# Third norm's first tiles turned through DRAM, and the first routed tiles' rows turned and signalled earlier

## The chip, the cores and the metric

The kernel runs on one core of one Trainium2 chip. The metric is the device time of one execution in microseconds; before the change it was 700.5 us in the median of three runs (699.7 to 701.65).

## What is computed

The input x has 16 x 64 = 1024 tokens of 512 numbers; a context of the same shape goes with it. Four blocks follow each other, each added to x:

```python
x = x + _L0_xattn_ref(_layernorm(x), ctx, ctx)            # linear attention, heads of 8 channels
x = x + _L0_ffn_ref(_layernorm(x), U1, V1, U2, V2, b1, b2) # low rank 128, inner width 1376
x = x + _L1_xattn_ref(_layernorm(x), ctx, Wq, Wk, Wv, Wo)  # 16 heads, 4 key/value heads of 96
x = x + _L1_ffn_ref(_layernorm(x), gate_w, bias, Wg, Wu, Wd, Sg, Su, Sd)
# the last one: scores = sigmoid(x @ gate_w.T) + bias; the best 4 of 16 experts of each token,
# weights normed to sum 1; out = sum over them of w * (silu(x@Wg.T) * (x@Wu.T)) @ Wd.T,
# plus a shared expert silu(x@Sg.T) * (x@Su.T) @ Sd.T
```

All is fp32. The experts have an inner width of 256.

## The kernel before

The 1024 tokens are 8 tiles of 128 rows (j = 0 to 7); x stays in SBUF as `xr`. One Python list, `prog`, holds all steps up to the routed experts in one order (lines 282 to 400), and each engine walks it and issues its own part of each step. So the order within each engine is written by hand, and semaphores join the engines.

The **second attention** is 32 units, n = 0 to 31, two per batch (lines 369 to 393). Unit n has on TensorE: the scores `s(n)` (8 matmul records, L1366), one large piece (a q projection `q`, an output projection half `op0`/`op1` of L1397, or a shared-expert piece `sh_gu`), the transposes `t(n-1)` of the probabilities (L1195), and `pv(n-2)` (L1382). VectorE has in it the largest score (L1038, L1040), `pn(n)` (L852, L853), the copies of q (L1029) and of pv (L1054, L1056). ScalarE has the exponentials (L746) and the copy of the transposes (L668). TensorE's pv(n) waits until VectorE has copied pv(n-1).

Once a tile j of x is final after `op1`, the **third norm** starts beside these units, placed by the table WAY (lines 353 to 357): `ln_stat` (VectorE L943, L944, then GpSimd's root, L562, L563), `ln_z` (VectorE writes the normed rows to one of two `zrow` buffers, L1001), `ln_t` (TensorE turns them in four 128x128 transposes, ScalarE copies them to `zT`, L668), `gate` (TensorE's scores for 16 experts), `gate_v` (VectorE's choice of the best four, L1078 to L940), and `place` (TensorE's running counts, then VectorE's slot numbers, L1108 to L1110). With the slot numbers GpSimd scatters the four copies of each row from `zrow` to `slot_rows` in DRAM (L601, four indirect DMAs for a tile), and writes token ids and weights to `slots` (L569, four more).

The **second norm** has another way to the same layout (lines 491 to 500 and 1003 to 1008): SyncE stores `zrow` to DRAM, loads it again in four quarters into `zquad`, and VectorE's 32x32 block transposes finish it (L1007).

After unit 31 come the last norms, the shared expert's products (`sh_gu`, `sh_d`; VectorE adds each of the eight `sh_d` to `xr`, L1130), and the tables of the routing, which ScalarE copies to `tab` (L790). Then come some 36 **routed tiles** of 128 slots. For each one the rows are loaded from `slot_rows` by four DMAs (`load_block`, L425; for tile 0 `load_first_block`, L431), turned by VectorE (`turn`, L925), and go through gate and up, a transpose, and down on TensorE; GpSimd adds the result to the output by an indirect DMA (L635).

SyncE's queue at that handover holds, in order: the first block's four loads, the wait for the load table, the wait for `tab`, the four loads of block 1, the two signals `s_w` that say that the weights of the first two experts are there (L530, L531), the eight stores of the output, and the loads of further experts. TensorE's first routed tile (`gate_up(0)`) waits for `s_w` and for the first turn. VectorE has turn 0 ahead of the add of `sh_d` 6 and turn 1 ahead of the add of `sh_d` 7 (L1126, L1127). TensorE waits for `tab` ahead of the last shared product, `sh_d` 7.

Of the kernel before, what the change touches and what calls it, by code (L numbers as in the profile page):

```python
# [29 lines left out]
PIECES = EW // D  # L30
EARLY = 4
WARM = 12
EPS = 1e-5
# [3 lines left out]
def build(nc, x_d, ctx_d, ctxT_d, cst_d, u1_d, v1_d, u2_d, v2_d, b1_d, b2_d,  # L37
# [10 lines left out]
    with ExitStack() as stack:  # L48
# [155 lines left out]
        s_x1 = sem("x1_done")  # L204
        s_z = sem("z_done")
        s_zst = [sem(f"second_norm_stored{i}") for i in range(2)]
        s_zld = sem("second_norm_loaded")
# [132 lines left out]
        for i, u in enumerate(lat_units[0][2:]):  # L340
# [7 lines left out]
            if i in (1, 3, 4):  # L348
# [3 lines left out]

        tail_of = ((10, 1, "ln_z"), (11, 2, "ln_t"), (12, 1, "gate"), (13, 1, "place"))
        WAY = [((7, 0, "op0"), (9, 0, "op1"), (9, 1, "ln_stat")) + tail_of,
               ((7, 0, "op0"), (8, 0, "op1"), (9, 1, "ln_stat")) + tail_of,
               ((6, 0, "op0"), (7, 0, "op1"), (7, 1, "ln_stat"), (8, 1, "ln_z"), (9, 2, "ln_t"), (9, 1, "gate"),
# [12 lines left out]
        for n in range(NU + 1):  # L369
            if n < NU:  # L370
                prog.append(("s", n))
            prog += [("gate_v", step[1]) for step in prog[since:] if step[0] == "gate"]
            since = len(prog)
            if n == 14:
                prog.append(("gate_b", 0))
            if n < len(lat_units[1]):
                prog.append(("kv", lat_units[1][n]))
            for j in BESIDE.get(n, ()):
                prog.append(("sh_gu", j))
            if n < NU:  # L380
                prog.append(("pn", n))
            q, r = n // 8, n % 8
            if q < 3 and r % 2 == 0:
                prog.append(("q", q + 1, r // 2))
            way(n, 0)
            if 1 <= n <= NU:
                prog.append(("t", n - 1))
            way(n, 2)
            if 2 <= n <= NU + 1:
                prog.append(("pv", n - 2))  # L390
            way(n, 1)
            if n == 13:
                prog.append(("front",))
# [6 lines left out]
                 ("sh_d", 4), ("sh_d", 5), ("sh_d", 6), ("sh_d", 7)]  # L400

        def order(kinds):
            return {step: i for i, step in enumerate(p for p in prog if p[0] in kinds and p[:2] != ("ln_t", 2))}

# [16 lines left out]

        def load_block(eng, block_of, par, landed):

            for b in range(4):
                eng.dma_start(xrow[b * QD:(b + 1) * QD, par, :].rearrange("p (a e) -> p a e", a=4),  # L425
                              quads_d[bass.ds(block_of, 1), b, :, :, :].rearrange("x j a e -> (x j) a e")).then_inc(landed, 16)
# [22 lines left out]
        def _(sp):  # L449
# [86 lines left out]
            with sp.Fori(2, loads) as o:  # L536
# [118 lines left out]
        def _(act):  # L655
# [15 lines left out]
            for step in prog:  # L671
# [18 lines left out]
                elif kind == "a_t":  # L690
# [3 lines left out]
                    copied(step, ekT[:, j % 2, :])  # L694
                elif kind == "ln_t" and step[1] != 2:

# [103 lines left out]
            def x_load(i, par):  # L800
# [3 lines left out]
                load_block(act, block_of, par, s_gx[par])  # L804

            act.wait_ge(s_tabl, 1)
            act.wait_ge(s_tab, 1)
            tail = act.value_load(head[0:1, 4:5], min_val=28, max_val=TILES - 3)
# [32 lines left out]
        def _(dve):  # L841
# [104 lines left out]
            for step in prog:  # L946
# [39 lines left out]
                elif kind == "ln_z":  # L986
# [5 lines left out]
                    if n >= 2:  # L992
                        old = [p for p in prog if p[0] == "ln_z"][n - 2]
                        if old[1] == 2:
                            dve.wait_ge(s_zst[old[2] % 2], 16 * (old[2] // 2 + 1))
                        else:
# [6 lines left out]
                elif kind == "ln_t" and step[1] == 2:  # L1003
                    j = step[2]
                    dve.wait_ge(s_zld, 64 * (j + 1))
                    dve.wait_ge(s_pt, j // 4 + 1)
                    dve.transpose(zT[:, :, j * P:(j + 1) * P].rearrange("p k (a j) -> p a k j", a=4),  # L1007
# [110 lines left out]
                elif kind == "sh_gu" and step[1] >= EARLY and step[1] % 2:  # L1118
                    i = step[1]
                    a = i // 2  # L1120
                    dve.wait_ge(s_hsil, a + 1)
                    dve.wait_ge(s_hg, i + 1)
                    dve.tensor_tensor(zs[:, a, :], shared_bank(i), shg[a % 2], ALU.mult).then_inc(s_hz, 1)
                elif kind == "sh_d":
                    j = step[1]
                    if j >= J - 2:  # L1126
                        turn(j - (J - 2), j % 2)  # L1127
                    dve.wait_ge(s_hd, j + 1)
                    dve.wait_ge(s_x3, j + 1)
                    dve.tensor_tensor(xr[:, j, :], shared_down(j), xr[:, j, :], ALU.add).then_inc(s_x4, 1)  # L1130
# [42 lines left out]
        def _(pe):  # L1173
# [24 lines left out]
            def normed(layer, j):  # L1198

                if layer == 2:  # L1200
                    pe.wait_ge(s_zt2, j + 1)
                else:
# [18 lines left out]
            for step in prog:  # L1221
# [28 lines left out]
                elif kind == "kv":  # L1250
# [36 lines left out]
                elif kind == "ln_t" and step[1] != 2:  # L1287
                    n = LNN[("ln_z", *step[1:])]
# [338 lines left out]
```

## Time and profile before

| | |
|---|---|
| median of three runs | 700.5 us |
| the profiled execution | 706.84 us, its span 704.7 us |
| TensorE busy | 678.4 us, 96% |
| VectorE, ScalarE, GpSimd busy | 346.1, 193.4, 176.4 us |
| chain that ended last | TensorE 80%, VectorE 7%, DMA 6% |
| mean granted TensorE clock | 0.991 |

The first 76 us hold the first attention, then the low-rank network runs to about 158 us, the projections to 194 us, the units of the second attention from 194 to 445 us, the shared expert to 489 us, and the routed tiles from 492 us on. Times are counted from the first instruction of the span. A DMA row of a queue gives the time for issuing, not for the transfer.

### The profile page before, as it was taken

Reading aid. Unit: us, or ns where it says so; the run is one execution under the profiler, and the core shown is the slowest. Engines: PE = TensorE matmul, PEld = TensorE weight load, DVE = VectorE, ACT = ScalarE, POOL = GpSimd, SP = SyncE. Lnnn points to the kernel's source line nnn. Section 1 sums busy time; section 2 is a strip of 40 time slices with the busy share of each in tenths; the row PEclk is TensorE's granted clock in tenths of the full one; section 3 lists DMA queues with packets and bytes.
Section 4 is the critical chain, followed back from the end, with each engine's and each line's share of the span. In section 5 each row is a group of like instructions: output and inputs, shape, how many; then the busy total and the mean of one; then the engine's idle time right before and its main releaser. Section 6 shows DMA issues by size and latency. Waiting matters only on the chain.

```text
span 704.7 us, 9742 instructions
## 1 busy us (share of the span) xinstructions
PE 678.4 (96%) x2460; PEld 403.3 (57%) x2461; DVE 346.1 (49%) x838; ACT 193.4 (27%) x543; POOL 176.4 (25%) x226
## 2 busy tenths in 40 slices
PE   9999999999999999999999999997999999999991
PEld 6555444446777776777776785674444444444440
DVE  3999232533344456576675767455333333333330
ACT  5452422222254332333333242220111111111110
POOL 2354210100000000013513314255033333433332
PEclk9999999999999999999999999999999999999997
DMA  9999998123310100001104105313767757868544
GB/s 338 408 421 420 422 421 331 45 75 134 116 50 0 57 34 0 1 21 41 60 2 150 60 2 170 129 75 88 265 165 136 168 98 180 187 137 233 94 65 58
DMA packets 60403, 103.19 MB, mean 146 GB/s; under 512 B 7200, under 2 KB 32544, under 8 KB 59712
## 3 DMA queue, kind: packets, MB, share of 16 engines
q1 hardware_dynamic: 30608, 73.61, 28.3%
q0 software_dynamic: 8816, 18.00, 12.7%
q10 hardware_dynamic: 20944, 11.15, 5.5%
q8 instruction: 18, 0.29, 0.2%
q14 instruction: 17, 0.14, 0.1%
HBM read 46.60 MB, written 56.26 MB: 146 GB/s over the span
## 4 chain that ended last, share of the span: by engine, by line
PE 80%; DVE 7%; DMA 6%; issue 2%; POOL 1%; ACT 1%; ACTq 1%; POOLq 1%; DVEq 0%; SPq 0%; another core or an unknown queue 0%
PE ps L1207 47%; PE ps L1397 12%; DMA out<-rq,sidx 5%; PE ps L1366 4%; PE ps L1382 4%; PE ps L1195 3%; DVE rq L975 3%; PE ps L1313 3%; PE ps L1314 3%; PE ps L1323 3%; PE ps L1335 1%; DMA xr<-in_x 1%; DVE st L943 1%; ACTq L425 1%; DVE zrow L1001 1%
## 5 line engine op out<-in xcount | busy, mean ns | idle before, releaser
L1207 PE MATMUL ps<-kv,rq 128*128 x432 | 194.1, 598 | 4.1 <-DVE rq L925 3.5
L1207 PE MATMUL ps<-zT,r 128*128 128x256 f32 (+1 forms) x552 | 132.6, 395 | 1.5 <-ACT kv L708 1.4
L1207 PEld LDWEIGHTS ps<-kv,rq 128*128 128x128 f32 x432 | 79.6, 191 | 92.0 <-issue 91.4
L1207 PEld LDWEIGHTS ps<-zT,r 128*128 128x128 f32 x552 | 103.4, 190 | 25.4 <-issue 12.0
L1397 PE MATMUL ps<-r 128*128 128x512 f32 x192 | 85.1, 593 | 0.0
L635 POOL DMA_INDIRECT out<-rq,sidx x36 | 56.7, 1574 | 112.0 <-DMA out<-rq,sidx 81.4
L562 POOL TENSOR_SCALAR ve<-mv 128x1 f32<-128x1 f32 x32 | 7.2, 224 | 292.6 <-DVE mv L944 292.6
L746 ACT ACTIVATE r<-ps,snm 128x128 f32<-128x128 f32 x128 | 45.3, 366 | 83.3 <-DVE snm L1040 79.8
L1134 DVE TENSOR_TENSOR rq<-ps,rq 128x256 f32<-128x256 f32 x36 | 15.3, 424 | 96.8 <-ACT rq L798 93.8
L1397 PEld LDWEIGHTS ps<-r 128*128 128x128 f32 x192 | 35.2, 190 | 38.3 <-issue 38.3
L798 ACT ACTIVATE rq<-ps 128x256 f32<-128x256 f32 x36 | 13.8, 384 | 126.5 <-PE ps L1207 105.9
L1145 DVE TENSOR_SCALAR rq<-ps,wts 128x512 f32<-128x512 f32 x36 | 27.0, 750 | 33.3 <-PE ps L1207 13.1
L601 POOL DMA_INDIRECT slot_rows<-zrow,sloti x32 | 33.5, 1046 | 35.0 <-DVE sloti L1110 26.8
L1029 DVE COPY rq<-ps 32x256 f32<-32x256 f32 x48 | 20.5, 427 | 41.5 <-PE ps L1207 41.0
L1016 DVE SCALAR_TENSOR_TENSOR rq<-ps,r,rq 128x512 f32<-128x512 f32 (+1 forms) x22 | 16.4, 749 | 40.3 <-ACT rq L727 40.3
L668 ACT COPY r<-ps 128x512 f32<-128x512 f32 x40 | 23.4, 586 | 45.3 <-PE ps L1195 42.7
L1366 PE MATMUL ps<-kv,rq 96*128 96x128 f32 x256 | 34.8, 279 | 0.0
L1382 PE MATMUL ps<-r,kv 128*96 128x256 f32 x128 | 32.9, 379 | 1.3 <-DVE r L1056 1.3
L569 POOL DMA_INDIRECT slots<-tokw,sloti x32 | 31.3, 977 | 10.4 <-issue 9.2
L1366 PEld LDWEIGHTS ps<-kv,rq 96*128 96x128 f32 x256 | 32.6, 192 | 1.4
L1054 DVE COPY r<-ps 96x192 f32<-96x192 f32 x64 | 19.8, 349 | 19.8 <-PE ps L1382 19.2
L1056 DVE COPY r<-ps 32x128 f32<-32x128 f32 x96 | 27.5, 287 | 1.3
(176 smaller groups left out, 843.3 us busy)
## 6 DMA issues: line engine op xcount, KB each, us to landing
slot_rows<-rq SPq DMA_DIRECT2D x4, 8192.0 KB, 50.2
kv<-in_experts SPq DMA_DIRECT2D x54, 256.0 KB
rq<-slot_rows ACTq DMA_DIRECT2D x136, 64.0 KB
r<-in_Wq SPq DMA_DIRECT2D x1, 3072.0 KB, 10.3
r<-in_Wo SPq DMA_DIRECT2D x2, 1536.0 KB, 6.4
r<-in_ctx SPq DMA_DIRECT2D x8, 256.0 KB, 8.3
xr<-in_x SPq DMA_DIRECT2D x8, 256.0 KB, 8.4
second_norm_rows<-zrow SPq DMA_DIRECT2D x8, 256.0 KB, 2.1
```

The costliest lines, as they stand in the source:

```text
L569: pool.indirect_dma_start(out=id_d.rearrange("a (b c) -> (a b) c", c=2), out_offset=bass.IndirectOffsetOnAxis(ap=sloti[:, j, k:k + 1], axi ...
L601: pool.indirect_dma_start(out=slot_d, out_offset=bass.IndirectOffsetOnAxis(ap=sloti[:, j, k:k + 1], axis=0), in_=zrow[:, LNN[("ln_z", 3, j ...
L635: pool.indirect_dma_start(out=out_d, in_=ylast[:, par, :] if last else yrow[:, par, :], in_offset=None, out_offset=bass.IndirectOffsetOnAx ...
L668: act.copy(dst, ps[:, n % 2, :] if len(dst.shape) == 2 else ps[:, n % 2, :].rearrange("p (k t) -> p k t", k=KC)).then_inc(s_trc, 1)
L746: e = act.activation(prob[:, n % 2, u, :], ps[:, 2 + n % 2, u * P:(u + 1) * P], ACT.Exp, bias=snm[:, n % 4, u:u + 1], scale=SCALE, accum_o ...
L975: link(dve.reciprocal(srec, ps[:, 5, :]))
L1056: c = dve.tensor_copy(dst[HD:P, :, t, :], src[32 * t:32 * t + 32, :, 3, :])
L1145: dve.tensor_scalar(ylast[:, par, :] if last else yrow[:, par, :], ps[:, 6 + par, :], wts[:, bass.ds(col, 1)], None, ALU.mult).then_inc(s_ ...
L1207: mm = pe.matmul(out, lhs(k), rhs(k), start=(k == 0), stop=(k == n - 1))
L1366: mm = pe.matmul(ps[:, 2 + n % 2, u * P:(u + 1) * P], qT[0:HD, q % 2, b % 4, h0:h0 + 2, :].rearrange("p h s -> p (h s)"), kT[0:HD, g, b, : ...
L1382: mm = pe.matmul(ps[0:HD, 6, 256 * g:256 * g + 256], v[:, b, c0:c0 + HD], probT[:, n % 2, 256 * g:256 * g + 256], start=True, stop=True)
L1397: mm = pe.matmul(ps[:, 7, :], oT[:, j % 2, m, :], wo[:, m, :], start=(m == 0), stop=(m == NQT - 1))
```

## The change

Third norm, tiles 0 to 4 (`TURNED = 5`): they go by DRAM and VectorE as the second norm does. VectorE writes the normed rows twice, once to `zrow` for GpSimd's scatter and once, with the 128-byte pieces in another order, to `zquad`. SyncE stores `zquad`, loads it again in quarters, and VectorE transposes it. The five TensorE transposes groups and ScalarE's five copies are gone. In the table, `ln_t`, `gate` and `place` of these tiles stand one unit later; `front` and `gate_b`, too. `gate` 4 and `gate` 5 now both stand in unit 29, their `gate_v` in unit 30. Tiles 0 to 3 of it stand on SyncE's queue ahead of the wait for all of q and the load of the shared weights, tile 4 behind it.

Handover: SyncE gives the two `s_w` signals before it waits for `tab`; of block 1 it loads two quarters, and ScalarE loads the other two on its own queue, ahead of its first `x_load`; SyncE reads the number of expert loads only behind the output stores. VectorE has turn 0 ahead of the add of `sh_d` 4.

```diff
+TURNED = 5
-        tail_of = ((10, 1, "ln_z"), (11, 2, "ln_t"), (12, 1, "gate"), (13, 1, "place"))
+        turned_of = ((10, 1, "ln_z"), (12, 1, "ln_t"), (13, 1, "gate"), (14, 1, "place"))
...
-            if n == 14:
+            if n == 15:
                 prog.append(("gate_b", 0))
...
-            if n == 13:
+            if n == 14:
                 prog.append(("front",))
...
+        def by_dram(step):
+            return step[0] == "ln_t" and (step[1] == 2 or step[1] == 3 and step[2] < TURNED)
...
             def turn_rows(j):
-                sp.wait_ge(s_z, LNN[("ln_z", 2, j)] + 1)
-                sp.dma_start(zrow_d[j % 2], zrow[:, LNN[("ln_z", 2, j)] % 2, :]).then_inc(s_zst[j % 2], 16)
+                z = LNN[("ln_z", 2 + j // J, j % J)]
+                sp.wait_ge(s_z, z + 1)
+                if j >= J:
+                    sp.wait_ge(s_zp, j - J + 1)
+                sp.dma_start(zrow_d[j % 2], zrow[:, z % 2, :] if j < J else zquad[:, :]).then_inc(s_zst[j % 2], 16)
...
             load_wo(1)
+            for j in range(4):
+                turn_rows(J + j)
             sp.wait_ge(s_q, 4 * G)
             sp.dma_start(wsh, ws_d).then_inc(s_ws, 16)
+            turn_rows(J + 4)
...
             load_first_block(sp)
-            sp.wait_ge(s_tabl, 1)
-            loads = sp.value_load(head[0:1, 2:3], min_val=TOPK, max_val=E)
-            sp.wait_ge(s_tab, 1)
-            load_block(sp, sp.value_load(tab[0:1, 1:2], min_val=0, max_val=P), 1, s_gx[1])
             for i in range(2):
                 sp.wait_ge(s_wdma[i], 16 * PIECES)
                 sp.sem_inc(s_w, 1)
+            sp.wait_ge(s_tab, 1)
+            load_block(sp, sp.value_load(tab[0:1, 1:2], min_val=0, max_val=P), 1, s_gx[1], range(2))
             for j in range(J):
                 sp.wait_ge(s_x4, j + 1)
                 sp.dma_start(out_d[j * P:(j + 1) * P, :], xr[:, j, :]).then_inc(s_out, 16)
-            sp.wait_ge(s_tab, 1)
+            sp.wait_ge(s_tabl, 1)
+            loads = sp.value_load(head[0:1, 2:3], min_val=TOPK, max_val=E)
...
+            act.wait_ge(s_tab, 1)
+            for k in range(TOPK):
+                act.wait_ge(s_zs[k], 16 * J)
+            load_block(act, act.value_load(tab[0:1, 1:2], min_val=0, max_val=P), 1, s_gx[1], range(2, 4))
...
+                    if layer == 3 and j < TURNED:
+                        dve.wait_ge(s_zt2, J + j)
+                        dve.tensor_scalar(zquad[:, :].rearrange("p (b k i) -> p k b i", b=4, k=KC),
+                                          xr[:, j, :].rearrange("p (k b i) -> p k b i", b=4, k=KC),
+                                          mv[:, col, 0:1], rstd[:, col:col + 1],
+                                          ALU.subtract, ALU.mult).then_inc(s_zp, 1)
...
                     j = step[1]
-                    if j >= J - 2:
-                        turn(j - (J - 2), j % 2)
+                    if j == J - 4:
+                        turn(0, 0)
+                    if j == J - 1:
+                        turn(1, 1)
                     dve.wait_ge(s_hd, j + 1)
```

TensorE's `normed` waits for the VectorE transposes (`s_zt2`) where a tile goes by DRAM, and for ScalarE's copy elsewhere; VectorE's `ln_t` waits for the loads of the tile.

## Rows read from the trace of the kernel before

**Rows 1.** The page: busy time of each engine, its share of the span, instructions.

```profile
PE 678.4 (96%) x2460; PEld 403.3 (57%) x2461; DVE 346.1 (49%) x838; ACT 193.4 (27%) x543; POOL 176.4 (25%) x226
```

**Rows 2.** Windows: each engine's busy time (instructions), granted clock, DMA share, GB/s.

```profile
330.00:360.00 30.00, 30.00 (x151) 22.77 (x150) 20.66 (x65) 10.64 (x42) 8.89 (x10) 1.00 0.09 36
492.00:498.00 6.00, 5.78 (x10) 2.53 (x11) 1.80 (x3) 0.35 (x1) 0.60 (x1) 0.72 0.93 327
```

**Rows 3.** Waits of TensorE, 440 to 560 us: total, times, longest.

```profile
PE ps L1207 <- DVE rq L925: 3.5, 1, 3.5
PE ps L1382 <- DVE r L1056: 1.3, 1, 1.3
```

**Rows 4.** Chain, 340 to 350 us: start, duration, what (t and ln_t together).

```profile
347.33 0.87 PE ps L1195 x8
```

**Rows 5.** By line: ns least/median/most, first and last start; landings of L494, L499.

```profile
L1007 DVE STREAM_TRANSPOSE zT<-zquad x8: 697/702/712, 139.5 to 195.7; 128x512 f32<-128x512 f32 x8
L1001 DVE TENSOR_SCALAR zrow<-xr,mv,rstd x24: 534/546/1267, 35.8 to 460.3; 128x512 f32<-128x512 f32 x24
DMA to landing us min/median/max: 2.0/2.1/2.2
DMA to landing us min/median/max: 1.8/1.9/2.9
```

**Rows 6.** Timeline of VectorE, units 29 to 31: start, duration, line, operation.

```profile
425.68 0.17 DVE L1078 TENSOR_SCALAR gsc<-gsc 128x16 f32<-128x16 f32 x1
428.29 0.44 DVE L940 TENSOR_SCALAR tokw<-top,wsum 128x4 f32<-128x4 f32 x1
433.56 0.69 DVE L1038 TENSOR_REDUCE smx<-ps 128x4 f32<-128x512 f32 x1
439.51 0.89 DVE L1056 COPY r<-ps 32x128 f32<-32x128 f32 x3
443.21 0.59 DVE L1001 TENSOR_SCALAR zrow<-xr,mv,rstd 128x512 f32<-128x512 f32 x1
```

**Rows 7.** Timeline of TensorE, there: start, duration, line, operation, idle before.

```profile
440.54 1.07 PE L1382 MATMUL ps<-r,kv 128*96 128x256 f32 x4 [1.26 <-DVE r L1056]
445.77 0.60 PE L1195 MATMUL ps<-cst,zrow 128*128 128x128 f32 x4
```

**Rows 8.** Timeline of GpSimd, there: scatters of tile 5, root of tile 6.

```profile
433.81 0.96 POOL L601 DMA_INDIRECT slot_rows<-zrow,sloti  x1 [3.31 <-DVE sloti L1110]
438.07 0.96 POOL L601 DMA_INDIRECT slot_rows<-zrow,sloti  x1 [0.30 <-issue]
441.43 0.23 POOL L562 TENSOR_SCALAR ve<-mv 128x1 f32<-128x1 f32 x1 [2.39 <-DVE mv L944]
```

**Rows 9.** Timeline of all engines at the handover, 480 to 496 us.

```profile
480.16 1.77 SPq L431 DMA_DIRECT2D rq<-slot_rows  x4
481.58 7.11 PE L1207 MATMUL ps<-r 128*128 128x512 f32 x16 [0.44 <-issue]
483.49 0.19 ACT L790 CAST tab<-ps 6x48 int32<-6x48 f32 x1 [9.05 <-remote]
486.96 3.94 SPq L425 DMA_DIRECT2D rq<-slot_rows  x4
489.87 1.45 DVE L1130 TENSOR_TENSOR xr<-ps,xr 128x512 f32<-128x512 f32 x2 [7.08 <-PE ps L1207]
491.24 0.70 DVE L925 STREAM_TRANSPOSE rq<-rq 128x512 f32<-128x512 f32 x1
494.10 0.71 DVE L925 STREAM_TRANSPOSE rq<-rq 128x512 f32<-128x512 f32 x1 [1.59 <-DMA rq<-slot_rows]
```

**Rows 10.** Chain, 480 to 706 us: start, duration, what.

```profile
501.26 3.45 PE ps L1207 x8
684.75 4.90 DMA out<-rq,sidx
693.15 1.57 POOL out L635
```

More of the change, by code:

```diff
@@ L205, in build @@
         s_z = sem("z_done")
+        s_zp = sem("z_permuted")
         s_zst = [sem(f"second_norm_stored{i}") for i in range(2)]
@@ L351, in build @@
         NU = 2 * B
-        tail_of = ((10, 1, "ln_z"), (11, 2, "ln_t"), (12, 1, "gate"), (13, 1, "place"))
-        WAY = [((7, 0, "op0"), (9, 0, "op1"), (9, 1, "ln_stat")) + tail_of,
-               ((7, 0, "op0"), (8, 0, "op1"), (9, 1, "ln_stat")) + tail_of,
+        turned_of = ((10, 1, "ln_z"), (12, 1, "ln_t"), (13, 1, "gate"), (14, 1, "place"))
+        WAY = [((7, 0, "op0"), (9, 0, "op1"), (9, 1, "ln_stat")) + turned_of,
+               ((7, 0, "op0"), (8, 0, "op1"), (9, 1, "ln_stat")) + turned_of,
                ((6, 0, "op0"), (7, 0, "op1"), (7, 1, "ln_stat"), (8, 1, "ln_z"), (9, 2, "ln_t"), (9, 1, "gate"),
@@ L400, in build @@
                  ("sh_d", 4), ("sh_d", 5), ("sh_d", 6), ("sh_d", 7)]
+        def by_dram(step):
+            return step[0] == "ln_t" and (step[1] == 2 or step[1] == 3 and step[2] < TURNED)
         def order(kinds):
-            return {step: i for i, step in enumerate(p for p in prog if p[0] in kinds and p[:2] != ("ln_t", 2))}
+            return {step: i for i, step in enumerate(p for p in prog if p[0] in kinds and not by_dram(p))}
         TRN = order(("a_t", "ln_t", "t", "gate", "front", "place", "count"))
@@ L420, in load_expert, with load_block @@
                              we_d[bass.ds(expert, 1), :, c * D:(c + 1) * D].rearrange("a p n -> (a p) n")).then_inc(landed, 16)
-        def load_block(eng, block_of, par, landed):
-            for b in range(4):
+        def load_block(eng, block_of, par, landed, parts=range(4)):
+            for b in parts:
                 eng.dma_start(xrow[b * QD:(b + 1) * QD, par, :].rearrange("p (a e) -> p a e", a=4),
@@ L694, in _ @@
                     copied(step, ekT[:, j % 2, :])
-                elif kind == "ln_t" and step[1] != 2:
+                elif kind == "ln_t" and not by_dram(step):
                     copied(step, zT[:, :, step[2] * P:(step[2] + 1) * P])
@@ L995, in _ @@
                             dve.wait_ge(s_zst[old[2] % 2], 16 * (old[2] // 2 + 1))
-                        else:
+                        elif not by_dram(("ln_t", *old[1:])):
                             dve.wait_ge(s_tr, TRN[("ln_t", *old[1:])] + 1)
@@ L1002, in _ @@
                                       ALU.subtract, ALU.mult).then_inc(s_z, 1)
-                elif kind == "ln_t" and step[1] == 2:
-                    j = step[2]
-                    dve.wait_ge(s_zld, 64 * (j + 1))
-                    dve.wait_ge(s_pt, j // 4 + 1)
+                    if layer == 3 and j < TURNED:
[4 more added lines that the diff above has]
+                                          ALU.subtract, ALU.mult).then_inc(s_zp, 1)
+                elif by_dram(step):
+                    j = step[2]
+                    dve.wait_ge(s_zld, 64 * (J * (step[1] - 2) + j + 1))
+                    if step[1] == 2:
+                        dve.wait_ge(s_pt, j // 4 + 1)
+                    else:
+                        dve.wait_ge(s_q, 4 * (j // 2) + 4)
+                        dve.wait_ge(s_pr, len(KVN))
                     dve.transpose(zT[:, :, j * P:(j + 1) * P].rearrange("p k (a j) -> p a k j", a=4),
@@ L1198, in normed @@
             def normed(layer, j):
-                if layer == 2:
-                    pe.wait_ge(s_zt2, j + 1)
+                if by_dram(("ln_t", layer, j)):
+                    pe.wait_ge(s_zt2, J * (layer - 2) + j + 1)
                 else:
@@ L1286, in _ @@
                               lambda k: weights[1][:, k, :], KC).then_inc(s_pr, 1)
-                elif kind == "ln_t" and step[1] != 2:
+                elif kind == "ln_t" and not by_dram(step):
                     n = LNN[("ln_z", *step[1:])]
```

1 line of the change is left out of this document (removed).

## The prediction

> **What bounds the kernel now.** I read the page's busy times first: TensorE is busy 96% of the span, the next engine 49% [rows 1]. So only two things can move the time: TensorE work that goes or comes, and the few places where TensorE stands. The windows by stage say where the second kind is. A window in the middle of the second attention has TensorE busy for 30.00 of 30 us, beside VectorE at 20.7 and ScalarE at 10.6 [rows 2]: TensorE sets the pace there, and VectorE has about a third of its time free. The waits of TensorE after 440 us name two stalls: 1.3 us for a copy of pv (L1056), and 3.5 us for the first routed turn (L925) [rows 3].
>
> The second one is the larger target, so I read its surroundings in the timeline [rows 9]. The four last shared products run from 481.58 to 488.69. The first routed product starts at 492.22 (turn 0 ends at 491.94, the timeline has it at 491.24 for 0.70). Turn 0 stands on VectorE behind the adds of `sh_d` 4 and 5, and VectorE, idle for 7.08 us, got to these only at 489.87, though the first of the products should by the records be done some 2 us after 481.58. SyncE gives the `s_w` signals behind its four loads of block 1: the loads were issued from 486.96 to 490.90, though `tab` was there at 483.68. These four loads took 3.94 us to issue where the four of the first block took 1.77. Whatever delayed both engines there, both things that TensorE needs were queued behind it. After the stall the granted clock was 0.72 in the window 492 to 498 [rows 2], a mean over the upper level (2.4 GHz) and the lower (1.2 GHz), and TensorE had stood for 3.5 us before it fell.
>
> **The change, part by part.**
>
> *Third norm, TensorE.* Eight transposes, four of `t` and four of `ln_t`, take 0.87 us of the chain [rows 4], so a tile's four take 0.435 us. Five tiles: -2.2 us, in a stage where TensorE never stands, so all of it counts. The copies that ScalarE loses were hidden.
>
> *Third norm, VectorE.* Each of five tiles adds one more normed write and one transpose. The transpose is 0.70 us; the write to `zrow` is 0.55 us [rows 5]. No row has the write with the other order of pieces: I take 0.55 us (same count of elements, contiguous pieces), at most the 1.27 us of the slowest of the 24 [rows 5], at least 0.53. So 1.25 us for a tile, 6.2 us in all. A tile has four units, some 31 us of TensorE, where VectorE has over 9 us free [rows 2]; that hides it on average. The fullest unit becomes n = 18 (as 22): the gate's choice, 3.05 us (L1078 at 425.68 to the end of L940 at 428.73 [rows 6]), moves to where the q copies and both writes are. It overfills that unit by 2 to 3 us. The next unit holds only scores, probabilities and pv copies, and TensorE has its 5-us piece before it needs pn: nothing. If that cover were gone, each of the four such units would cost up to 2 us.
>
> *The round trip.* The store lands 2.1 us after its issue, the loads 1.9 us [rows 5], with issuing in between some 6 us. VectorE's transpose comes two units (15 us) after the write and the gate one unit after that: nothing. On SyncE's queue the wait stands ahead of the load of the shared weights; tile 3's rows are written in unit 22, where q is finished too, and the shared weights are needed three units later: nothing. Behind VectorE's new wait stands the reduction of the next scores, so a late landing would reach TensorE; from 6 us to 15 us there is room.
>
> *The end of the units.* `gate_v` 4 and 5 both come in unit 30. TensorE's place of 5 needs the second one, and gets it about 0.8 us before its turn. But the reduction of the scores 31 (433.56 before) moves behind two slot computations, and the chain reduction, exponential, pn 31, copies of pv 29 moves with it. The pv copies end at 440.40 before (L1056 [rows 6]), and TensorE, which waits for them, starts at 440.54 after 1.26 us of idle [rows 7]: I put this copy 0.55 us later. Then GpSimd: its four scatters of tile 5 start at 433.81, and the root of tile 6 at 441.43 finds it free [rows 8]. After the change the scatters of 4 and 5, eight at 1.3 us, start near 434.4 and end near 445, the root follows, and `ln_z` 6 (443.21 before [rows 6]) ends near 446.9. TensorE's transposes of tile 6 started at 445.77 [rows 7], now 446.3 with the delay above: another 0.55 us. Together +1.1 us, bounds 0 and 3 (if VectorE comes a further 2 us late). The third norm nets -1.1 us.
>
> *Handover.* Turn 0 now waits only for its rows, which were issued at 480.16 to 481.93; at the worst landing of block 1 (issued until 490.90, turned at 494.10 [rows 9], so 3.2 us) they are there by 486. `s_w` comes before the wait for `tab`. So `gate_up(0)` can start when the last shared product ends, at 488.69: -3.5 us. It runs 3.45 us (eight products [rows 10]), to 492.1. `gate_up(1)` needs turn 1, still ahead of the add of `sh_d` 7. Two loads each on two queues take 1.97 us to issue at the measured 3.94 us for four: from 486.96 to 488.9, landed 3.2 us later at 492.1, turned at 492.8, TensorE at 493.1. A new stall of 0.9 us. Its bounds: nothing if the issue is as quick as the first block's 1.77 us, 3 us if the delay stays as large as it was. With the short idle the clock should not fall: 6 us at 0.72 [rows 2] lost 1.7 us, which come back. The handover nets -3.5 + 0.9 - 1.7 = -4.3 us, bounds 0 and -5.2. The output stores and the later expert loads move with it; the two further loads on ScalarE stand ahead of its first silu, which is idle till then.
>
> *Sum.* -1.1 - 4.3 = -5.4 us on the profiled execution, 706.84 to 701.4 us. The median of the runs lies 6.3 us below that execution. Is the handover's stall in the timed runs? In the chain the last scatter-add starts at 693.15, and the one before that of which the landing is seen took 4.90 us [rows 10]; so work ends at about 698, and 6.7 us of the span and 2.1 us around it hold no work. The 6.3 us fit there. They would also fit the stall, the clock and 0.6 us of small gaps (5.8 us), if these came from the profiling. I take the first: 700.5 - 5.4 = **695.1 us**.
>
> The Trainium skill bears on this choice (page "Runtime: NRT & Kernel Launch", section "The ~15µs preamble/postamble breakdown"): it states a gap of about 6.2 us, between 6.02 and 6.67 over 14 kernels, between a profile's total time and the reported one. Here the difference is 6.34 us, so the trace agrees, and by that rule the timed runs hold the stall and the result would be 695.1 us; if the rule did not hold here, 699.4 us.
>
> **The rivals.**
>
> *The stall is not in the timed runs.* Then only the third norm's -1.1 us counts: **699.4 us**, 0.16% less, no measurable change. For it: the odd delay at 482 to 490 us hits VectorE and SyncE together while their own work was ready, and nothing in the kernel explains it. Against it: the room at the end of the span.
>
> *The delay follows.* The same trouble holds the loads of block 1, and TensorE stops in front of `gate_up(1)` instead, for 3 us, with the fall of the clock: the handover gives back 0.5 us and the kernel ends at **698.9 us**. For it: those loads were landed only at 494.10. Against it: half go by another queue.
>
> *VectorE becomes the bound of the units.* It ends on the other side. Place: the units that now hold the second write and the transpose. It decides once VectorE's excess in a unit exceeds the 5 to 6 us of TensorE's large piece that cover it, by a landing that comes late or by a write of 1.27 us. With 2 us lost for each of five tiles (+10), -2.2 us for the transposes and the handover's stall alone (-3.5 + 0.9, the clock gives nothing back), that is +5.2 us, **705.7 us**. Against it: VectorE is busy 20.7 of 30 us.
>
> **How the numbers follow.** Forecast 0.50; stall not in the timed runs 0.23; delay follows 0.14; VectorE the bound 0.13. The likeliest one's own range is 693.3 to 697.5. The range of 8 in 10 is 693 to 701: it takes in the second and third cases, and leaves out the fourth. 0.3% is 2.1 us, about what a measurement here can tell from no change. Faster by more: nearly all of the first (0.48), 0.04 of the second, 0.06 of the third, 0.58. Within: 0.01 + 0.16 + 0.06 + 0.01 = 0.24. Slower: 0.12 of the fourth, 0.03 of the second, 0.02 of the third, 0.01 of the first, 0.18.
>
> **What the profile after would show.** Right: 20 fewer L1195 transposes from zrow, L1007 with 13 transposes at 0.70 us; TensorE without a wait for L925 before the first routed product; turn 0 before 488; `s_w` no longer behind L425; a granted clock of 1.00 in the 6 us after the handover; the wait before pv 30 near 1.8 us and one of about half a microsecond at the transposes of tile 6. Wrong: a TensorE wait for L1007's tile or for L1038's chain within units 10 to 28; a wait of 3 us before the second routed tile; or all as forecast in the trace and no change of the median, which would say that the profile's stall is its own.

## The result and the profile after

| | before | after |
|---|---|---|
| median, same chip | 700.7 us (699.7 to 702.55, 6 runs) | 703.6 us (702.4 to 707.43, 6 runs) |
| ratio, 95% interval | | 1.005 (1.0036 to 1.0064) |
| the profiled execution | 706.84 us, span 704.7 us | 702.4 us, span 700.6 us |

The kernel became 0.5% slower; 695.1 us had been forecast. The profiled execution of after is 4.4 us shorter than the one of before, but the latter lies 4.3 us above the highest of before's timed runs and was no ordinary one. So after is set below beside a second profile of before, called e0, which took 700.7 us. After's profiled execution is the quickest of its six (702.4 us, median 703.6), so its trace holds 1.7 of the 2.9 us between the medians. Medians in this document leave out the few executions that lie over 1.5% above the quickest of the same kernel.

The page's busy times of after answer to [rows 1]: TensorE has 20 instructions less, VectorE ten more.

```profile
PE 675.8 (96%) x2440; PEld 401.7 (57%) x2441; DVE 351.4 (50%) x848; ACT 190.4 (27%) x538; POOL 175.4 (25%) x226
```

The windows of after (columns as in [rows 2]). The first and third are those of [rows 2]: in the middle of the units nothing has changed for TensorE, and the handover has the full clock. The second, in unit 29, is new: a clock of 0.76 as the mean of 7.22 us.

```profile
330.00:360.00 30.00, 30.00 (x147) 22.52 (x146) 21.10 (x65) 10.12 (x40) 8.92 (x10) 1.00 0.16 53
417.68:424.90 7.22, 6.67 (x36) 5.29 (x35) 3.46 (x12) 2.54 (x10) 0.00 (x0) 0.76 0.00 0
492.00:498.00 6.00, 6.00 (x16) 2.67 (x15) 1.56 (x3) 1.03 (x3) 0.60 (x1) 1.00 0.92 259
```

TensorE's waits in after, 190 to 560 us (total, times, longest). The 3.5 us of [rows 3] are gone; 1.9 us for `zrow` and 0.6 us for ScalarE's copy are new.

```profile
PE ps L1221 <- DVE zrow L1015: 1.9, 1, 1.9
PE ps L1408 <- DVE r L1080: 1.3, 1, 1.3
PE ps L1233 <- ACT r L679: 0.6, 1, 0.6
...
```

The same view of e0, the ordinary execution of before, has no wait for a turned tile either. Its 2.3 us of "issue" (idle time without a wait that the profile shows) lie behind the first routed product.

```profile
PE ps L1207 <- issue: 2.3, 2, 1.3
PE ps L1382 <- DVE r L1056: 1.3, 1, 1.3
```

The timeline of TensorE in after shows where the new idle times lie, and the start of the last shared products (483.04) and of the routed ones (490.01).

```profile
418.12 1.03 PE L1408 MATMUL ps<-r,kv 128*96 128x256 f32 x4
419.70 1.97 PE L1233 MATMUL ps<-gw,zT 128*128 128x16 f32 x16 [0.55 <-ACT r L679]
...
440.66 1.07 PE L1408 MATMUL ps<-r,kv 128*96 128x256 f32 x4 [1.26 <-DVE r L1080]
...
447.94 0.66 PE L1221 MATMUL ps<-cst,zrow 128*128 128x128 f32 x4 [1.89 <-DVE zrow L1015]
...
483.04 7.13 PE L1233 MATMUL ps<-r 128*128 128x512 f32 x16
490.01 7.03 PE L1233 MATMUL ps<-kv,rq 128*128 x16
```

In e0 the same two steps come at 480.83 and 487.80, back to back; turn 0 was done there at 485.87.

```profile
480.83 7.13 PE L1207 MATMUL ps<-r 128*128 128x512 f32 x16
487.80 7.03 PE L1207 MATMUL ps<-kv,rq 128*128 x16
496.04 3.69 PE L1207 MATMUL ps<-kv,rq 128*128 x8 [0.99 <-issue]
```

That is the result in one subtraction. At the last shared products after is 2.2 us later than e0 (483.04 against 480.83), and 2.4 us counted from the first scores of the second attention (194.14 in e0, 193.97 in after). The terms in between: 2.2 us less for the transposes; 0.55 us of idle at the gates, and behind it 3.42 us (421.44 to 424.86) at half clock, which lose 1.7 us; 1.9 us at the transposes of tile 6. These sum to +2.0 us (to 0.1), so 0.4 us is not accounted for. Behind that point after wins back 1.1 us on TensorE (its last product ends at 686.47, e0's at 685.38).

**The gates.** TensorE's two gates of unit 29 (the expert scores of tiles 4 and 5) wait for ScalarE's copy of `t` 28. ScalarE and VectorE there, in after:

```profile
415.42 0.70 DVE L1031 STREAM_TRANSPOSE zT<-zquad 128x512 f32<-128x512 f32 x1
416.15 0.69 DVE L1062 TENSOR_REDUCE smx<-ps 128x4 f32<-128x512 f32 x1
```

```profile
417.08 0.37 ACT L757 ACTIVATE r<-ps,snm 128x128 f32<-128x128 f32 x1 [3.56 <-DVE snm L1064]
...
418.93 0.62 ACT L679 COPY r<-ps 128x512 f32<-128x512 f32 x1
```

VectorE's transpose of tile 4 stands ahead of the reduction of scores 29; the exponentials 29 wait for that; the copy of `t` 28 stands behind the exponentials on ScalarE; and the gates need the PSUM tile which this copy empties.

**Tile 6.** GpSimd in after, the first two of the four scatters of tile 5: each waits for the landing of an earlier one, and the root of tile 6 starts at 446.34 where [rows 8] has 441.43.

```profile
440.13 0.96 POOL L612 DMA_INDIRECT slot_rows<-zrow,sloti  x1 [1.13 <-DMA slot_rows<-zrow,sloti]
442.56 0.96 POOL L612 DMA_INDIRECT slot_rows<-zrow,sloti  x1 [1.47 <-DMA slot_rows<-zrow,sloti]
...
446.34 0.24 POOL L573 TENSOR_SCALAR ve<-mv 128x1 f32<-128x1 f32 x1
```

**The shared weights.** SyncE in after gives their load (L526) behind tile 3's round trip, at 377.33; in the first profile of before it went at 371.23. It landed 8.3 us later, at 385.6, and TensorE's first product of `sh_gu` stands at 386.46: 0.9 us to spare, and no wait in this execution.

```profile
375.49 1.80 SPq L508 DMA_DIRECT2D zquad<-second_norm_rows  x4
377.33 0.48 SPq L526 DMA_DIRECT2D r<-in_shared  x1
```

### The profile page after: what moved, and what is told of

Same layout as the page of the kernel before. It is cut to its first block, busy times and chain, and to the rows that moved or that the text cites. A ratio compares the mean times of both kernels' runs of the same rounds, so it can differ in the third digit from the quotient of the medians.

```text
span 700.6 us, 9746 instructions
## 1 busy us (share of the span) xinstructions
PE 675.8 (96%) x2440; PEld 401.7 (57%) x2441; DVE 351.4 (50%) x848; ACT 190.4 (27%) x538; POOL 175.4 (25%) x226
## 4 chain that ended last, share of the span: by engine, by line
PE 73%; DVE 9%; DMA 8%; issue 3%; POOL 3%; ACT 1%; ACTq 1%; POOLq 1%; SPq 0%; DVEq 0%
PE ps L1233 44%; PE ps L1423 10%; DMA out<-rq,sidx 5%; PE ps L1392 4%; DVE rq L989 3%; PE ps L1408 3%; PE ps L1339 3%; PE ps L1340 3%; PE ps L1221 3%; PE ps L1349 3%; POOL slot_rows L612 1%; DMA slot_rows<-zrow,sloti 1%; PE ps L1361 1%; DMA xr<-in_x 1%; DVE st L957 1%
## 5 line engine op out<-in xcount | busy, mean ns | idle before, releaser
L580 POOL DMA_INDIRECT slots<-tokw,sloti x32 | 30.9, 965 | 10.5 <-issue 9.2
L939 DVE STREAM_TRANSPOSE rq<-rq 128x512 f32<-128x512 f32 x36 | 25.3, 702 | 8.7 <-DMA rq<-slot_rows 8.7
```

The lines of the kernel that those rows point to most:

```text
L580: pool.indirect_dma_start(out=id_d.rearrange("a (b c) -> (a b) c", c=2), out_offset=bass.IndirectOffsetOnAxis(ap=sloti[:, j, k:k + 1], axi ...
L939: dve.transpose(xT[:, par, :].rearrange("p (k a j) -> p a k j", k=KC, a=4), xrow[:, par, :].rearrange("p (a k i) -> p a k i", a=4, k=KC)). ...
```

## The experiments

The kernels ran in five sets, each on one chip and beside runs of before on it. In two of them before ran at 705.9 and 705.6 us, in three at 700.5 to 701.5 us; sets 2 and 5 ran on chips of the same number, 13. Only ratios, and medians of one set, are compared.

| set (before) | kernel | median us | ratio, 95% interval |
|---|---|---|---|
| 1 (701.51) | e1 handover alone | 701.1 | 0.9988 (0.9976 to 1.0) |
| | e2 third norm alone | 703.31 | 1.0024 (0.9998 to 1.0049) |
| | e3 after, tile 4 old | 700.84 | 0.9987 (0.9974 to 1.0001) |
| 2 (705.94) | e4 root of 6 first | 704.65 | 0.9979 (0.9952 to 1.0006) |
| | e5 shared weights first | 707.78 | 1.0034 (1.0009 to 1.006) |
| | e6 before, gate 4 late | 708.11 | 1.0029 (1.0 to 1.0058) |
| | e7 four tiles, weights first | 700.07 | 0.9934 (0.991 to 0.9958) |
| 3 (705.58) | e8 after | 707.12 | 1.0012 (0.9991 to 1.0034) |
| | e9 = e7, old handover | 705.12 | 0.9997 (0.9978 to 1.0015) |
| | e10 = e1 | 701.13 | 0.9948 (0.9927 to 0.9968) |
| | e11 = e4 and e5 | 704.72 | 0.9983 (0.9967 to 0.9999) |
| 4 (700.84) | e12 = e11, turn behind | 698.89 | 0.9967 (0.9955 to 0.998) |
| | e13 = e7 | 698.47 | 0.9961 (0.9948 to 0.9974) |
| | e14 = e1 | 700.02 | 0.9997 (0.9986 to 1.0009) |
| 5 (700.5) | e15 after | 702.63 | 1.0028 (1.0014 to 1.0042) |
| | e16 = e11 | 700.07 | 0.9989 (0.9975 to 1.0002) |
| | e17 = e12 | 698.42 | 0.9971 (0.9957 to 0.9986) |

**e0: before, a second profile.**

> The kernel before, unchanged, for a second profile. Theory A (the execution whose trace I read was an unusual one, 6.1 us above the median, and the stall of 3.5 us with the low clock behind it is not in an ordinary execution): 699.7 to 702.5 us, no TensorE wait for L925 ahead of the first routed product, at most 0.5 us idle there, clock 1.00 from 490 to 500 us. Rival B (the stall is ordinary and the profile's time differs for another reason): again a wait near 3.5 us and about 706 us.

700.7 us, span 698.8 us. Shown above: no wait for turn 0, and the clock is at its upper level till 687.9 us. The stall of the first profile is not in every execution of before. ScalarE's copy of `tab` shows the difference early: its idle time before it is 9.05 us in [rows 9] and 6.47 us here.

```profile
480.93 0.19 ACT L790 CAST tab<-ps 6x48 int32<-6x48 f32 x1 [6.47 <-PE ps L1445]
```

**e1: the handover's part alone; e2: the third norm's part alone.**

The diffs show one place of each part; the rest of the part is undone in the same way.

```diff
 # e1, against after
...
-        turned_of = ((10, 1, "ln_z"), (12, 1, "ln_t"), (13, 1, "gate"), (14, 1, "place"))
+        tail_of = ((10, 1, "ln_z"), (11, 2, "ln_t"), (12, 1, "gate"), (13, 1, "place"))
...
 # e2, against after
-                    if j == J - 4:
-                        turn(0, 0)
-                    if j == J - 1:
-                        turn(1, 1)
+                    if j >= J - 2:
+                        turn(j - (J - 2), j % 2)
...
```

> The kernel before with the handover's part alone (signals before the table wait, block 1 split over two queues, turn 0 ahead of the add of sh_d 4). Theory A (no stall in ordinary executions): ratio 0.998 to 1.001. Rival B (stall ordinary, the handover saves it): 0.993 to 0.996. Rival C (the handover itself is what costs the 3 us): 1.003 to 1.006.

> The change's third-norm part alone, handover as before. Theory A (TensorE gains 2.2 us of transposes and loses 0.6 us idle and 1.7 us of clock at the pair of gates in unit 29, and 1.9 us ahead of the transposes of tile 6, with some executions losing more): ratio 1.002 to 1.006, about that of the full change. Rival C: 0.997 to 0.999.

Each part alone has before's code in place of the other part. The handover is worth 0.1% here. The third norm's part costs 1.8 us by the medians, with an interval that just holds no change. In e2's profile (span 704.0 us) a third loss shows beside the two of after, the wait for the shared weights. TensorE's waits in e2:

```profile
PE ps L1229 <- DMA r<-in_shared: 3.4, 1, 3.4
PE ps L1217 <- DVE zrow L1013: 1.6, 1, 1.6
...
```

The answer on that tile in e2: issued at 377.4 as in after, landed 12.6 us later where it was 8.3 us in after.

```profile
L526 SPq DMA_DIRECT2D r<-in_shared x1: 501/501/501, 377.4 to 377.4; - x1
...
DMA to landing us min/median/max: 12.6/12.6/12.6
```

**e3: after with tile 4 in the old way.**

```diff
-TURNED = 5
+TURNED = 4
...
+        tail_of = ((10, 1, "ln_z"), (11, 2, "ln_t"), (12, 1, "gate"), (13, 1, "place"))
...
-               ((7, 0, "op0"), (8, 0, "op1"), (9, 1, "ln_stat")) + turned_of,
+               ((7, 0, "op0"), (8, 0, "op1"), (9, 1, "ln_stat")) + tail_of,
...
-            turn_rows(J + 4)
```

> The full change, but tile 4 as before (ScalarE's copy and TensorE's transposes, its gate in unit 28, four tiles by DRAM). Theory A (all of the loss is made where gate 4 and gate 5, and place 4 and place 5, fall together): the waits of 0.6 us in unit 29 and of 1.9 us at the transposes of tile 6 are gone, the low clock in unit 29 too; four tiles give 1.7 us: ratio 0.996 to 0.999. Rival D (the second write and the VectorE transposes of every tile cost as well, spread over the units): 1.000 to 1.004.

With tile 4 the wait at the gates, the half clock behind it and the wait at tile 6 all went, and the loss with them. Two things are undone in one here (VectorE's transpose of tile 4, and its gate and place a unit later), so e4 to e6 take them apart.

**e4: the root of tile 6 ahead of the scatters of tile 5.**

`place_rows(j)` holds the four scatters of a tile; for tile 5 it is called behind the root of tile 6.

```diff
...
                     root(J * step[1] + step[2])
+                    if step[1:] == (3, J - 2):
+                        place_rows(J - 3)
...
-                elif step[0] == "place":
...
+                elif step[0] == "place" and step[1] != J - 3:
+                    place_rows(step[1])
```

> The full change, but GpSimd does the root of tile 6 ahead of the scatters of tile 5. Theory A (the root stood behind eight scatters): the wait of 1.9 us ahead of the transposes of tile 6 falls to under 0.3 us; the idle and the low clock at the pair of gates stay; about 1.7 us less than the full change, ratio about 1.002. Rival (the wait has another cause, DMA landing or VectorE): unchanged, 1.005.

**e5: the shared weights' load ahead of tile 3's round trip.**

```diff
-            for j in range(4):
+            for j in range(3):
                 turn_rows(J + j)
             sp.wait_ge(s_q, 4 * G)
             sp.dma_start(wsh, ws_d).then_inc(s_ws, 16)
+            turn_rows(J + 3)
```

> The full change, but the load of the shared weights stands ahead of tile 3's round trip on SyncE's queue. Theory A (the load was put off by 6.1 us, so that in some executions TensorE waits for it, 3.4 us in the one of the third-norm part alone): the load is issued near 370 us and landed near 378 us, no execution has that wait, the scatter of the times shrinks (highest under 705), ratio 1.002 to 1.004. Rival (the scatter comes from elsewhere): highest again 705 to 712, ratio 1.005.

In e4 the wait for `zrow` is gone from TensorE's list, and GpSimd has the root ahead of the second four scatters:

```profile
445.57 0.23 POOL L573 TENSOR_SCALAR ve<-mv 128x1 f32<-128x1 f32 x1 [2.77 <-DVE mv L962]
445.88 0.57 POOL L574 TENSOR_TENSOR rstd<-ve,half 128x1 f32<-128x1 f32 x1
446.64 1.07 POOL L594 DMA_INDIRECT slot_rows<-zrow,sloti  x1 [0.19 <-issue]
```

In e5 the load is given at 369.87 and nothing waits for it; the wait at tile 6 is still there (1.6 us). Both keep the one at the gates, here 2.0 us, and in both TensorE waits 1.9 us for the turned rows of the second routed tile, with 3.4 us at half clock behind it. TensorE's waits in e4:

```profile
PE ps L1237 <- ACT r L683: 2.0, 1, 2.0
PE ps L1237 <- DVE rq L943: 1.9, 1, 1.9
...
```

So each edit took away its own wait. The medians are not where they were expected: e4 is at 0.998 of before in place of 1.002, and e5 at 1.003 with a highest time of 709.86 us where under 705 was expected, so the late load is not all that scatters the times. The full change was not run in set 2, so what each edit is worth by itself isn't told; e4, without the wait at tile 6, lies 3.1 us under e5.

**e6: before, with only gate 4 and place 4 a unit later.**

```diff
-               ((7, 0, "op0"), (8, 0, "op1"), (9, 1, "ln_stat")) + tail_of,
+               ((7, 0, "op0"), (8, 0, "op1"), (9, 1, "ln_stat"), (10, 1, "ln_z"), (11, 2, "ln_t"), (13, 1, "gate"), (14, 1, "place")),
```

> The kernel before with nothing by DRAM; only gate 4 and place 4 stand one unit later, beside gate 5 and place 5. Theory A (the table's move makes the loss, not the DRAM way): idle of about 0.5 us at the gates, the clock at half for 3.4 us behind them, 1.5 to 2 us of wait at the transposes of tile 6; together +3.5 us, ratio 1.004 to 1.006. Rival D (the loss comes from VectorE's added work and the DRAM traffic): ratio 0.999 to 1.002, clock 1.00.

The wait at tile 6 came (1.98 us): it belongs to the eight scatters in a row. The wait at the gates did not, so the pair of gates alone doesn't make it. ScalarE in e6 ends the copy of `t` 28 at 421.30, and TensorE's gates start at 421.53 without idle time:

```profile
418.83 0.37 ACT L746 ACTIVATE r<-ps,snm 128x128 f32<-128x128 f32 x1 [2.94 <-DVE snm L1040]
...
420.68 0.62 ACT L668 COPY r<-ps 128x512 f32<-128x512 f32 x1
```

```profile
419.80 0.60 PE L1195 MATMUL ps<-cst,r 128*128 128x128 f32 x4
...
421.53 1.85 PE L1207 MATMUL ps<-gw,zT 128*128 128x16 f32 x16
```

The exponentials 29 start 0.97 us ahead of `t` 28 in e6, and 0.16 us ahead of it in after (417.08, 417.24). The difference, 0.81 us, is about the transpose's 0.70. e12 tests this directly.

**e7: four tiles, tile 4 old, the shared weights first.** e3 and e5 together.

> Four tiles by DRAM, tile 4 as before, the shared weights' load ahead of tile 3's round trip, handover as changed. Theory A: none of the three losses, 1.7 us less of TensorE work: 0.9965 to 0.9985, at or under the run with the late load, with less scatter. Rival D (each tile by DRAM costs as much as it saves): 0.999 to 1.001.

0.9934 of before, the best of its set and lower than expected, and 4.6 us under the median of e4, which has tile 4 by DRAM and the late load. e9 and e10 ask if this set owes that to the handover.

**e8: the full change again; e9: e7 with the old handover; e10: e1 again; e11: e4 and e5 together.** They have the diffs above.

> The full change, unchanged, timed on the same chip as the next three. Theory A (TensorE loses in the pair of gates and ahead of the transposes of tile 6, sometimes at the shared weights): slower than before on a chip where the kernel before runs at 700 to 701 us (ratio 1.003 to 1.007), less so or equal on one where the kernel before itself is held up at the handover. Rival: 0.992 to 0.996, my first forecast.

> Four tiles by DRAM, shared weights' load ahead, but the handover as before. Theory A, if the handover gives nothing in ordinary executions: 0.997 to 0.999, like the four-tile kernel with the changed handover. Rival E (the gain of 0.66% of that kernel came from the handover, on a chip where late signals of TensorE are frequent): 0.998 to 1.001.

> The handover's part alone once more. Theory A: 0.998 to 1.001 where the kernel before runs at 700 to 701 us. Rival E: 0.993 to 0.997 where the kernel before runs at 704 us and more, since there the stall of the first profile is frequent and this part removes it.

> Five tiles by DRAM with two mends: root of tile 6 ahead of the scatters of tile 5, and the shared weights' load ahead of tile 3's round trip. Theory A: what remains of the loss is the idle of 0.5 us and more at the pair of gates with the clock at half for 3.4 us behind it: no wait for the transposes of tile 6 over 0.3 us, none for the shared weights, ratio 1.000 to 1.002. Rival (that part loses nothing): 0.996 to 0.999.

e8's profile (span 706.5 us) holds all three losses and a wait of 1.2 us before the second routed tile. TensorE's waits in e8:

```profile
PE ps L1233 <- DMA r<-in_shared: 2.7, 1, 2.7
PE ps L1233 <- ACT r L679: 2.0, 1, 2.0
PE ps L1221 <- DVE zrow L1015: 1.8, 1, 1.8
PE ps L1233 <- DVE rq L939: 1.7, 2, 1.2
...
```

e9 brings the stall of [rows 3] back, the same 3.5 us. TensorE's, ScalarE's and VectorE's rows at e9's handover repeat [rows 9]:

```profile
482.16 0.19 ACT L803 CAST tab<-ps 6x48 int32<-6x48 f32 x1 [9.10 <-remote]
...
488.53 1.46 DVE L1153 TENSOR_TENSOR xr<-ps,xr 128x512 f32<-128x512 f32 x2 [7.08 <-PE ps L1230]
...
490.85 6.68 PE L1230 MATMUL ps<-kv,rq 128*128 x11 [3.51 <-DVE rq L938]
```

And e10, the handover's part alone, gives 0.5% here against 0.1% in set 1 and 0.0% in set 4. So the stall is real, and it is frequent where before runs at 705 to 706 us; the new handover removes it there and finds next to nothing to remove elsewhere. The traces divide the same way: ScalarE's idle time before its copy of `tab` is 6.47 us in after, in e0 and in every profile of sets 1, 4 and 5, and 9.0 to 10.5 us in the first profile of before and in all eight of sets 2 and 3. The stall's 3.5 us and the 1.7 us lost at half clock behind it are 5.2 us, about what before runs longer there; before itself was not profiled in those sets.

e11 was expected at 1.000 to 1.002 with a wait of some 0.5 us for the gates; it has 0.9983, and the wait is 2.0 us. Its VectorE starts the copies of pv 26 at 414.80, though TensorE's products for it had ended at 413.00 and e12 has these copies at 413.43. Timeline of VectorE in e11:

```profile
414.80 0.62 DVE L1083 COPY r<-ps 96x192 f32<-96x192 f32 x2 [1.37 <-remote]
...
416.81 0.70 DVE L1036 STREAM_TRANSPOSE zT<-zquad 128x512 f32<-128x512 f32 x1
417.54 0.69 DVE L1067 TENSOR_REDUCE smx<-ps 128x4 f32<-128x512 f32 x1
```

TensorE's signal came 1.4 us late, all of the chain moved with it, and the wait grew from 0.55 to 2.0 us. A late signal and the transpose add up.

**e12: e11 with VectorE's transpose of tile 4 behind reduction 29; e13: e7 again; e14: e1 again.**

```diff
...
-               ((7, 0, "op0"), (8, 0, "op1"), (9, 1, "ln_stat")) + turned_of,
+               ((7, 0, "op0"), (8, 0, "op1"), (9, 1, "ln_stat"), (10, 1, "ln_z"), (13, 1, "gate"), (14, 1, "place")),
...
+            if n == 29:
+                prog.append(("ln_t", 3, 4))
...
```

The new step stands right behind the scores of unit 29.

> The five tiles with both mendings (root of tile 6 first, shared weights' load first), and VectorE's transpose of tile 4 (0.70 us) behind the reduction of scores 29 in place of ahead of it. Theory A (the gates of tile 4 wait because ScalarE's copy of t28 stands behind exponentials 29, and these are late by VectorE's transpose): reduction 29 and the exponentials start 0.7 us earlier, the wait for that copy goes (from 0.55 us) or shrinks to about 1.3 us where TensorE's signal is late too (from 2.0), and the ratio to before comes 0.1 to 0.3% under that of the same kernel without this edit (0.998), at 0.995 to 0.997. Rival: the wait is that of the late signal alone; it stays as long and the ratio stays at 0.998.

> Four tiles by DRAM and VectorE, tile 4 in the old way, shared weights' load first, new handover, once more beside the handover alone on the same chip. Theory A: four times 0.435 us less on TensorE and no new wait, so 1.7 us (0.25%) below the handover alone. Rival D (what TensorE is spared at the third norm comes back as another idle time): equal to the handover alone within 0.1%.

> The handover's part alone, third time, as the measure of the kernel above. Theory E (its gain is that of the chip: as large as the before kernel is held up there): ratio 0.999 if before runs near 701 us, 0.995 if it runs near 705.5. Theory A: in both cases 0.25% above the kernel with four tiles. Rival D: equal to it.

e13 (five executions) lies 1.6 us under e14 by the medians, 1.9 us with a 95% uncertainty of 1.0 by the means, where four tiles times 0.435 us give 1.7: what TensorE is spared at the third norm does reach the end. e12's waits hold neither the gates nor tile 6:

```profile
PE ps L1415 <- DVE r L1087: 1.5, 1, 1.5
PE ps L1240 <- issue: 1.0, 1, 1.0
...
```

But no late signal shows at that place in e12 either, so the edit and the set are mixed. Set 5 separates them.

**e15: after; e16: e11; e17: e12, in one set.**

> The full change once more, on one chip with the two kernels below. All theories: slower than before, at 1.002 to 1.006, with the wait for the copy of t28 (0.5 to 2 us).

> Five tiles with the root of tile 6 and the shared weights' load first. Theory A (VectorE's transpose ahead of reduction 29 makes the gates of tile 4 wait): still a wait of 0.5 to 2 us before the gates, at times the half clock behind it, 0.998 to 1.000 of before. Rival (that wait comes with the late signal alone, so only on the chips that have it): if before runs near 701 us here there is no such wait, and this kernel equals the next.

> The same with VectorE's transpose of tile 4 behind reduction 29. Theory A: no wait before the gates, or 0.7 us less of one, and 0.1 to 0.3% below the kernel above. Rival: equal to the kernel above, within 0.1%.

e15 repeats after: waits of 1.7 us at tile 6 and 0.57 us at the gates, with 3.4 us at half clock behind the latter, and 0.3 us for the shared weights. TensorE's gates in e16, and in e17, the transpose's place being the only difference:

```profile
419.79 1.93 PE L1238 MATMUL ps<-gw,zT 128*128 128x16 f32 x16 [0.56 <-ACT r L684]
```

```profile
419.56 1.93 PE L1240 MATMUL ps<-gw,zT 128*128 128x16 f32 x16
```

In e16 the clock was at half from 422.25 to 425.67; in e17 it never fell before 686 us. The medians differ by 1.65 us, the means by 1.2 with a 95% uncertainty of 1.0. The last shared products start at 481.05 and 479.51, and counted from the first scores (194.06, 194.46) e17 is 1.9 us quicker. From e15 to e16, the root and the shared weights first, the median falls by 2.6 us. With all three edits e17 has 698.42 us, 2.1 us less than before (1.0 to 3.0 by the interval of the ratio), and the five tiles bring their saving. e12 and e13 can't be told apart (698.89, 698.47): the fifth tile's 0.435 us is within the spread.

## Why the prediction was wrong, step by step

- **"I take the first" (the handover's stall is in the timed runs): failed**, and with it 4.3 of the 5.4 us. Of the 8.5 us between forecast and result these are the larger half; the rest is the third norm's part, -1.1 us forecast and +2.9 us by the medians if the handover gives nothing (+1.8 for that part alone in e2), and 0.2 us between the two medians of before. The choice rested on one profiled execution being 6.3 us above the median and on 6.7 us of room at the end of its span. e0 shows an execution of 700.7 us without the stall, with the same kind of end (last product at 685.38, span 698.8). The Trainium skill (page "Runtime: NRT & Kernel Launch", section "The ~15µs preamble/postamble breakdown") states a gap of some 6.2 us between a profile's total and the reported time. That is a gap between two numbers for one execution. The 6.34 us of the prediction lie between one execution and the median of others, which is another thing. What the runs have of the first kind is the time of an execution and its span: the time is 1.8 to 2.2 us above the span in each of the before runs of the five sets, in after's profile (702.4 against 700.6) and in the first profile of before (706.84 against 704.7). So the page's figure says nothing on this choice, and that the two agree to 0.2 us was chance.
- **The handover's mechanism: right.** Turn 0 at 487.04 in after, the routed products back to back, the clock 1.00 in the window 492 to 498. The new wait of 0.9 us before the second routed tile is not in after. Where the stall exists (set 3) the part gives 4.5 us by the medians (705.58 to 701.13), against 4.3 forecast, and e10 waits 0.7 us before the second routed tile.
- **Third norm, TensorE, -2.2 us: right in size**, as e17 shows with -2.1 us in all (the new handover included, worth 0.0 to 0.1% in the sets without late signals). VectorE: 13 transposes at a mean of 707 ns, and the write with the other order 541 ns against 0.55 taken. In 330 to 360 us TensorE again never stands.
- **"The shared weights are needed three units later: nothing": failed.** The load went 6.1 us later and left 0.9 us of room in after's profile; where it took longer to land TensorE waited: 0.3 us (e15, landed after 9.5 us), 3.4 us (e2, 12.6 us) and 2.7 us (e8, whose landing the trace does not have). The cover was measured in units and the landing of a load of 1.5 MB wasn't costed.
- **The end of the units, pv 30: +0.55 forecast, nothing came.** The wait is 1.26 us as in [rows 7].
- **Tile 6: the mechanism right, the term mis-sized.** 0.55 us forecast, 1.89 us measured. The scatters were taken as eight at 1.3 us; a scatter also waits until an earlier one has landed (1.13, 1.47 and 0.57 us in after), and the root came at 446.34, not at 445.
- **The gates: not foreseen.** Behind the transpose I named the reduction of the next scores and asked only if the landing could be late. Its 0.70 us by itself was enough, since the copy of `t` 28 had only 0.23 us of room (421.30 to 421.53 in e6): 0.55 us of idle and the half clock, 2.3 us together. That a short idle time leaves the clock alone, which the prediction took for the handover, did not hold here.
- **The rivals.** "The stall is not in the timed runs" was right in its cause and wrong in its sign, since it took over the -1.1 us of the third norm. "VectorE becomes the bound" was on the right side, but at the units of tiles 0 to 3 TensorE didn't wait for VectorE; it was one instruction ahead of another in unit 29. "The delay follows" is seen in sets 2 and 3: TensorE waits before the second routed tile for 0.7 us in e7 and e10, 1.1 to 1.2 in e8 and e11, and 1.9 in e4 and e5, there with 3.4 us at half clock behind it; the three microseconds of that rival were not reached.

Open: what delays TensorE's signals in sets 2 and 3, and what held up the load of the shared weights. GpSimd issues indirect DMAs in that stretch (374 to 385 us); that they slow the load was not tried, and they stand within 0.1 us at the same times in after, where it landed in 8.3 us, and in e2, where it took 12.6.

## What to carry to other kernels

Before forecasting that a stall will go, find out if the timed median holds it: one execution above all timed runs speaks for itself alone. When a step is moved ahead of others on a queue, cost each of those by its room, landing included, to the instruction that needs it: two waits of 0.6 and 1.9 us and 1.7 us lost at half clock used up a saving of 2.2, and a third wait of up to 3.4 us came in some executions. On an in-order engine place an added instruction behind the one that feeds the critical engine; moving a 0.7-us transpose by one place was worth 1.2 to 1.7 us.

## What was not expected of the hardware

- TensorE's products were done and the others learnt of it late: ScalarE's idle time before `tab` is 9.05 us in [rows 9] where 6.47 is ordinary, and VectorE starts the copies of pv 26 in e11 1.4 us late. All eight profiles of sets 2 and 3 have it at `tab`, none of the ten of sets 1, 4 and 5; sets 2 and 5 ran on chips of the same number.
- The clock fell to half for 3.4 us after 0.55 us of idle in after and after 0.56 in e16, for as long after 3.51 us in e9 and after 2.66 and 2.0 us in e8, and for 6.8 us after 1.99 in e4. It did not fall after 1.89 us in after (tile 6), 1.98 in e6, 2.00 in e11 and 3.37 in e2 (the shared weights), nor after the 1.3 to 1.5 us that TensorE waits before pv 30. The length of the idle time alone does not say if it falls, nor for how long.
- The same load of 1.5 MB, issued at 377.3 to 377.6 us in each case, landed 8.2 us later in e3, 8.3 in after, 9.5 in e15, and 12.6 in e2. Issued at 369.2 to 369.8 us, ahead of tile 3's round trip, it took 6.1 to 6.4 us in e7, e11, e12, e13, e16 and e17.
